# One ScalarE copy of 2048 half-words in place of a ScalarE and a VectorE copy, in the first attention of a macaron block

## The chip, the cores and the metric

The kernel runs on one core of a Trainium2 chip. The metric is the device time of one execution in microseconds (us), median of several runs. TensorE (PE in the profile) does the matmuls, VectorE (DVE), ScalarE (ACT) and GpSimd (POOL) the rest; SyncE (SP) issues most of the DMAs.

## The reference, cut to what matters

Two sequences of 1024 rows of 128 values go through two blocks, each a feed-forward, an attention and a feed-forward. The change lies in the attention of the first block: 16 heads of width 8, keys and queries turned by their position (rope), causal mask.

```
x = x + 0.5 * _L0_ffn_ref(_layernorm(x, axis=-1), ...)
x = x + _L0_attn_ref(_layernorm(x, axis=-1), L0_attn_W_KQV, L0_attn_W_O)    # here
x = x + 0.5 * _L0_ffn_ref(_layernorm(x, axis=-1), ...)
...
K, Q, V = to_heads(K), to_heads(Q), to_heads(V)
Q = _rope(Q, freqs)
K = _rope(K, freqs)
scores = jnp.einsum('bhqd,bhkd->bhqk', Q, K) / sqrt(d)
scores = jnp.where(causal, -jnp.inf, scores)
probs = jax.nn.softmax(scores, axis=-1)
heads = jnp.einsum('bhqk,bhkd->bhqd', probs, V)
```

## The kernel before, in words

The 32 heads of both sequences are worked on in 8 groups of 4 heads (`G` = 8, `key` or `g` is the group). Keys and queries are kept as 16-bit floats in `stacks`, a row of the sequence on each partition. For a group, a step `gkq` turns both with 16 TensorE transposes (line 1365), 8 for the keys into the first bank of a PSUM slot and 8 for the queries into the second. Each bank then holds 512 words of 4 bytes, that is 1024 values of 16 bits for each partition. The values leave for SBUF, to `KT` and `QT`, which lie side by side: ScalarE copies the keys (line 684, called at 793), VectorE the queries (line 1047).

After this come, for each group, 18 steps `gmax` (TensorE makes scores with queries as rows, line 1207, with the mask at line 1198; VectorE takes maxima by blocks, line 1054), one `gturn` (the maxima are turned, line 1376, and a DMA puts them among the rows of the turned queries), 18 steps `gexp` (scores with keys as rows, ScalarE takes the exponential, line 811), 9 steps `gweigh` (TensorE weighs the values, line 1156) and one `gheads`. ScalarE also saves the group's sum (`save_heads`, line 690).

Every step that needs PSUM takes the next slot of a ring of 3 slots of 2 banks (`RING`). Before it writes, TensorE waits until all the readers named in the step have read what the slot's user of three steps earlier left there. A few side steps have a bank of their own. The order of all steps is written out by hand in the string `ORDER`, where `a` is `gkq`, `m` `gmax`, `t` `gturn`, `e` `gexp`, `w` `gweigh`; every engine goes through it in this order, and nothing overtakes on an engine. It begins with `ammmmmmmmammm`. So `gkq` of group 0 is the first step, that of group 1 comes after 8 `gmax` of group 0, that of group 2 among `gmax` of group 1, and so on up to group 7. The steps `h` are the feed-forward parts and norms between the two attentions: `xt` (a transpose, copied out by ScalarE, line 684, and for some by VectorE, line 1032), `up` (line 1346; ScalarE takes a tanh, line 790, VectorE gates, lines 1042 and 1043) and others.

Some steps are preceded by idle matmuls that keep the clock up (`keep_clock`, line 1246, counts in `KEEP`). The first `gmax` of a group waits until both copies of its `gkq` are done.

After the first attention, from about 300 us on, the second attention (16 heads of width 64, in 16 pairs) and the last feed-forward parts follow in the same ring.

Of the kernel before, what the change touches and what calls it, by code (L numbers as in the profile page):

```python
# [10 lines left out]
F16 = mybir.dt.float16  # L11
# [15 lines left out]
G = B * H // GH  # L27
# [19 lines left out]
SETS = 3  # L47
# [97 lines left out]
def gated_steps(s, b):  # L145
    return (turned_norm_steps(s, b) + [("up", (s, b), (c, half), "AV") for c in range(HC) for half in range(2)]
            + [("down", (s, b), None, "V")])


def first_steps(b):  # L150
    rope = [[("rope", (b, half), k, "") for k in range(4)] for half in range(2)]
    return (int_ffn_steps(0, b) + turned_norm_steps(1, b) + [("qk", b, 0, "A")] + rope[0][:2] + [("v", b, None, "A")]
            + rope[0][2:] + [("qk", b, 1, "A")] + rope[1])


def middle_steps(b):
    return ([("acts", b, None, "A"), ("wo0", b, None, "V")] + int_ffn_steps(2, b) + gated_steps(3, b)
            + turned_norm_steps(4, b))


def streams():

    halves = [(i, u) for i in range(CH) for u in range(2)]
    return {
        "a": [("gkq", g, None, "AV") for g in range(G)],
        "m": [("gmax", g, at, "V") for g in range(G) for at in halves],
        "t": [("gturn", g, None, "A") for g in range(G)],
        "e": [("gexp", g, at, "A") for g in range(G) for at in halves],
        "w": [("gweigh", g, i, "") for g in range(G) for i in range(CH)],
        "g": [("gheads", g, None, "V") for g in range(G)],  # L170
        "Q": [("pq", p, None, "AV") for p in range(PAIRS)],
        "K": [("pk", p, None, "AV") for p in range(PAIRS)],
        "V": [("pv", p, None, "A") for p in range(PAIRS)],
        "M": [("max", p, i, "V") for p in range(PAIRS) for i in range(CH)],
        "T": [("turn", p, None, "AV") for p in range(PAIRS)],
        "E": [("exp", p, i, "A") for p in range(PAIRS) for i in range(CH)],
        "W": [("weigh", p, i, "") for p in range(PAIRS) for i in range(CH)],
        "S": [("sum", p, None, "A") for p in range(PAIRS - 1)],
        "O": [("wo", b, (0, (NP, WO_EARLY)[b], k), "V") for b in range(B) for k in range(WO_PARTS)],
        "h": (first_steps(1) + [("scale", 1, None, "V")]  # L180
              + [("wsplit", n, None, "") for n in range(3)] + middle_steps(0) + middle_steps(1) + gated_steps(5, 0)),
    }
# [12 lines left out]
    "MWMEMWMEEEKWWMEMWMEQThVEMSEMMWWWMEEMWWWMEEMWWMEEEMWWWTSEEEEWWWWEEEEEESWWOOOOEEWWWWWWW"  # L195
)
LEFT = {letter: iter(steps) for letter, steps in streams().items()}
PLAN = [next(LEFT[letter]) for letter in ORDER]
AT = {step[:3]: n for n, step in enumerate(PLAN)}
SLOT_NO = [0] + list(accumulate(int(bool(step[3])) for step in PLAN))  # L200
# [33 lines left out]
def read(e, *key):  # L234

    return READS[e][AT[key]]
# [15 lines left out]
def macaron_block_kernel(nc, x, w_kqv, w_o0, w_int, w_scale, bias, w_q, w_k, w_v, w_o1, w_gate, w_up,  # L252
# [3 lines left out]
    with ctx:  # L256
        def sb(name, shape, dt=F32):
            return ctx.enter_context(nc.sbuf_tensor(name, shape, dt))

        def sem(name):  # L260
            return ctx.enter_context(nc.semaphore(name))
# [10 lines left out]
        big = sb("big", [P, 16384])  # L272
# [42 lines left out]
               for at in (wkqv_s[0:2 * T, 2 * P:3 * P], turns[0:2 * T].rearrange("p w t d -> p (w t d)"))]  # L315
# [12 lines left out]
            "p h s d -> p (h s d)")  # L328
        KT, QT = ([big[:, 8192 + 1024 * r + 512 * w:8192 + 1024 * r + 512 * (w + 1)].bitcast(F16) for r in range(SETS)]
                  for w in range(2))  # L330
        spare = big[:, 15360:16384]
        mall = spare[:, 0:2 * GH * T * T].rearrange("p (r h t k) -> p r h t k", r=2, h=GH, t=T)
        mxn = spare[:, 512:576].rearrange("p (r h t) -> p r h t", r=2, h=GH)
# [31 lines left out]
        def slot_of(n):  # L365
            return ps[:, 6, :] if ON_SIDE[n] else banks(2 * (RING_NO.get(n, 0) % RING), 2)
# [12 lines left out]
        slot_filled, slot_act, slot_dve = sem("slot_filled"), sem("slot_act"), sem("slot_dve")  # L379
        slot_seen = {"A": slot_act, "V": slot_dve}  # L380
# [108 lines left out]
        def _(pool):  # L489
# [88 lines left out]
            g.memset(tops(1), SHIFT_TOP).then_inc(slots_set, 1)  # L578

            for n, (kind, key, arg, _) in enumerate(PLAN):  # L580
                if kind == "ln" and arg == 1:
                    s, b = key
# [94 lines left out]
        def _(act):  # L677
            a = nc.scalar
# [3 lines left out]
            def copy_out(n, dst, src):  # L682
                act.wait_ge(slot_filled, SLOT_NO[n] + 1)
                a.activation(dst, src, ACT.Copy).then_inc(slot_act, 1)  # L684
# [35 lines left out]
            def copy_heads(half):  # L720

                act.wait_ge(rope_sum, half + 1)
                for w, (at, (first, again)) in enumerate(((Ks, K_HIGH), (Qs, Q_HIGH))):
                    at = at[:, 0, :, heads[half]]
                    ins = a.activation(at[:, :, :, first], RA[half][:, :, 8 * w:8 * w + 8], ACT.Copy)
                ins.then_inc(high_done, 1)
                act.wait_ge(high_done, half + 1)
                for w, (at, (first, again)) in enumerate(((Ks, K_HIGH), (Qs, Q_HIGH))):
                    at = at[:, 0, :, heads[half]]
                    ins = a.activation(at[:, :, :, again], at[:, :, :, first], ACT.Copy)  # L730
                ins.then_inc(dups_done, 1)
# [9 lines left out]
            for n, (kind, key, arg, readers) in enumerate(PLAN):  # L741
                slot = slot_of(n)
# [47 lines left out]
                    a.activation(ffn_g[:, (2 * c + half) % 2], slot[:, 0:512], ACT.Tanh, scale=0.5 * W_SCALE).then_inc(slot_act, 1)  # L790

                if kind == "gkq":
                    copy_out(n, KT[key % SETS], slot[:, 0:512].bitcast(F16))
                    if key == 0:
                        copy_heads(1)
                        act.wait_ge(w_in, 16 * W_LOADS)
                        for k in range(3):
                            if k == 2:
                                act.wait_ge(wmax_ready, 2)
                            a.activation(ffn_h[:, k % 2], w_raw[k], ACT.Square,  # L800
                                         accum_out=wmax[1][:, k:k + 1]).then_inc(wmax_ready, 1)
# [59 lines left out]
        def _(dve):  # L861
            v = nc.vector
# [122 lines left out]
            for n, (kind, key, arg, readers) in enumerate(PLAN):  # L985
                slot = slot_of(n)
# [46 lines left out]
                if kind == "up":  # L1033
                    c, half = arg
                    dve.wait_ge(slot_act, READS["A"][n])
                    if arg == (0, 0):
                        dve.wait_ge(converted, 1)
                        before = last_before(n, "down")
                        if before is not None:
# [2 lines left out]
                    link(v.scalar_tensor_tensor(gate, gate, 1.0, slot[:, 0:512], ALU.add, ALU.mult))  # L1042
                    v.tensor_tensor(ffn_h[:, c, 512 * half:512 * half + 512], gate, slot[:, 512:1024],
                                    ALU.mult).then_inc(slot_dve, 1)
                if kind == "gkq":
                    dve.wait_ge(slot_filled, SLOT_NO[n] + 1)
                    v.tensor_copy(QT[key % SETS], slot[:, 512:1024].bitcast(F16)).then_inc(slot_dve, 1)
                if kind == "gmax":
                    i, u = arg
                    r = key % 2  # L1050
# [22 lines left out]
                if kind in ("pq", "pk"):  # L1073
                    r = key % SETS
# [3 lines left out]
                if kind == "max":  # L1078
                    r = key % 2
# [64 lines left out]
        def _(pe):  # L1144
# [57 lines left out]
            def group_scores(slot, pieces, u, still, moving, cut):  # L1202

                for q, (t, a0, a1, off) in enumerate(pieces):
                    for h in range(2):
                        rows = slice(HR * (2 * u + h), HR * (2 * u + h + 1))
                        ins = te.matmul(slot[:, 512 * h + off:512 * h + off + a1 - a0], still[rows, tile(t)],  # L1207
                                        moving[rows, a0:a1], start=q == 0, stop=cut is None and q == len(pieces) - 1)
                return ins if cut is None else cut_group(slot, u, cut)
# [78 lines left out]
            for n, (kind, key, arg, readers) in enumerate(PLAN):  # L1288
# [6 lines left out]
                slot = slot_of(n)  # L1295
# [70 lines left out]
                if kind == "gmax":  # L1366
                    i, u = arg
                    if (i, u) == (0, 0):
                        for e in "AV":
                            pe.wait_ge(slot_seen[e], read(e, "gkq", key, None))  # L1370
                    r = key % SETS
                    ins = group_scores(slot, M_PLACED[i], u, QT[r], KT[r], cutq0 if i in DIAGONAL else None)
                if kind == "gturn":
# [4 lines left out]
                if kind == "gexp":  # L1378
# [4 lines left out]
                    r = key % SETS  # L1383
# [21 lines left out]
                if kind == "max":  # L1405
                    r = key % SETS
# [9 lines left out]
                if kind == "exp":  # L1416
                    r = key % SETS
# [157 lines left out]
```

## Time and profile before

| | |
|---|---|
| time, median of 3 runs | 804.91 us (800.31 to 806.59) |
| the profiled execution's own time | 800.03 us |
| its span, first to last instruction | 798.2 us |
| mean granted clock of TensorE | 0.959 |
| busy: PE, DVE, ACT, POOL | 91%, 67%, 56%, 58% of the span |
| `gkq` steps | 8, from 35 to 243 us |

Durations below are of the one profiled execution. Its time is 1.8 us more than its span, and 4.88 us less than the median of the timed runs. The granted clock of TensorE is given as a share of 2.4 GHz: 0.5 is 1.2 GHz.

### The profile page before, as it was taken

To read this page: it belongs to the slowest core of one execution; us is meant where nothing else is said; L and a number is where in the kernel's file an instruction comes from. 1 tells how busy PE (TensorE), PEld (TensorE's weight loads), DVE (VectorE), ACT (ScalarE), POOL (GpSimd) and SP (SyncE) were. 2 spreads that over 40 slices of the span, in tenths; PEclk is the share of its full clock that TensorE was granted. 3 is DMA by queue.
4 is the path that set the end of the run, shared out by engine and by line. 5 is a ranking of instruction groups with operands and counts; after the bars stand their busy time and mean duration, and the time that the engine had idled before them with its cause. 6 is when DMAs were issued, how large, how long until landed. Compare 5 with 4: busy or idle time off the path is not lost.

```text
span 798.2 us, 21288 instructions
## 1 busy us (share of the span) xinstructions
PE 725.3 (91%) x9393; PEld 429.3 (54%) x9406; DVE 532.1 (67%) x704; ACT 450.9 (56%) x495; POOL 466.8 (58%) x367
## 2 busy tenths in 40 slices
PE   3667888888888899998999999999999999999997
PEld 1533454445335444554565565555776655676764
DVE  7699967889778765777675575556536556753037
ACT  2424769986575689555636655665444665546312
POOL 6815567600850300499968777877655986667840
PEclk9855989999899999999999999999999999999999
DMA  8000000000000000000001111001101101111110
GB/s 271 2 1 2 3 2 3 2 3 2 2 2 2 2 3 2 2 2 5 27 4 26 29 30 29 10 22 28 30 2 28 29 3 29 29 29 30 28 29 26
DMA packets 13223, 16.18 MB, mean 20 GB/s; under 512 B 3052, under 2 KB 10572, under 8 KB 13132
## 3 DMA queue, kind: packets, MB, share of 16 engines
q1 hardware_dynamic: 12556, 14.50, 6.3%
q8 instruction: 74, 1.21, 0.6%
q10 hardware_dynamic: 576, 0.33, 0.2%
q14 instruction: 17, 0.14, 0.1%
HBM read 13.26 MB, written 1.17 MB: 18 GB/s over the span
## 4 chain that ended last, share of the span: by engine, by line
PE 70%; DVE 17%; POOL 5%; ACT 5%; issue 3%; DMA 0%; ACTq 0%; POOLq 0%; DVEq 0%
PE ps L1228 19%; PE ps L1177 16%; DVE big L1054 9%; PE ps L1156 6%; PE ps L1398 5%; PE ps L1207 5%; PE ps L1435 3%; ACT Pr L811 3%; PE ps L1403 2%; PE ps L1352 2%; PE ps L1238 2%; POOL acts L672 1%; DVE moments L1004 1%; PE ps L1346 1%; PE ps L1318 1%
## 5 line engine op out<-in xcount | busy, mean ns | idle before, releaser
L1081 DVE TENSOR_REDUCE mxb<-ps 128x8 f32<-128x1024 f32 x144 | 173.3, 1222 | 90.4 <-PE ps L1228 61.3
L672 POOL TENSOR_TENSOR V0s<-V0s,Pr 128x1024 f32<-128x1024 f32 x77 | 182.1, 2365 | 62.7 <-ACT Pr L840 31.0
L1054 DVE TENSOR_REDUCE big<-ps 128x8 f32<-128x1024 f32 x144 | 168.9, 1218 | 27.9 <-PE ps L1207 16.6
L811 ACT ACTIVATE Pr<-ps,exp_scale 128x1024 f32<-128x1024 f32 x144 | 154.8, 1114 | 44.4 <-PE ps L1207 31.5
L840 ACT ACTIVATE Pr<-ps,exp_scale 128x1024 f32<-128x1024 f32 x112 | 119.5, 1114 | 90.3 <-PE ps L1228 72.9
L1228 PE MATMUL ps<-big 64*128 64x128 f16 (+2 forms) x2560 | 168.9, 259 | 0.7 <-DVE mxb L1081 0.4
L1207 PE MATMUL ps<-big 32*128 32x128 f16 (+2 forms) x1280 | 102.4, 279 | 35.7 <-DVE big L1054 22.2
L1228 PEld LDWEIGHTS ps<-big 64*128 64x128 f16 x2560 | 92.8, 94 | 71.6 <-issue 17.0
L1177 PE MATMUL ps<-Pr,V1s 128*64 128x128 f32 (+2 forms) x960 | 111.3, 371 | 0.0
L1207 PEld LDWEIGHTS ps<-big 32*128 32x128 f16 x1280 | 40.4, 95 | 108.5 <-DVE big L1054 53.1
L587 POOL TENSOR_TENSOR stats<-moments 128x8 f32<-128x8 f32 x9 | 1.9, 210 | 163.7 <-DVE moments L1004 163.7
L684 ACT ACTIVATE big<-ps 128x1024 f16<-128x1024 f32 (+3 forms) x63 | 51.9, 826 | 71.0 <-PE ps L1398 28.2
L672 POOL TENSOR_TENSOR acts<-acts,Pr 128x1024 f32<-128x1024 f32 x35 | 82.5, 2357 | 13.2 <-ACT wkqv_s L823 4.0
L1156 PE MATMUL ps<-Pr,V0s 128*18 128x128 f32 (+2 forms) x1280 | 82.1, 382 | 0.2 <-ACT Pr L690 0.2
L1177 PEld LDWEIGHTS ps<-Pr,V1s 128*64 128x64 f32 x960 | 56.0, 136 | 37.1 <-issue 24.7
L1077 DVE TENSOR_TENSOR big<-ps,big 128x1024 f16<-128x1024 f32 x32 | 39.1, 1223 | 34.4 <-ACT big L684 33.6
L1228 PE MATMUL ps<-big,shr_s 64*128 64x256 f16 (+2 forms) x384 | 55.8, 287 | 0.0
L518 POOL TENSOR_TENSOR big<-Pr,rec_b 128x1024 f32<-128x1024 f32 x15 | 35.5, 2363 | 17.6 <-DMA rec_b<-scratch_dram 7.5
L1398 PE MATMUL ps<-XT,wqkv 128*128 128x512 f16 x192 | 45.3, 380 | 0.0
L1156 PEld LDWEIGHTS ps<-Pr,V0s 128*18 128x18 f32 x1280 | 30.4, 100 | 20.2 <-issue 13.2
L840 ACT ACTIVATE V0s<-ps,exp_scale 128x1024 f32<-128x1024 f32 x22 | 24.5, 1114 | 18.2 <-PE ps L1218 17.0
L1398 PEld LDWEIGHTS ps<-XT,wqkv 128*128 128x128 f16 x192 | 17.6, 98 | 22.0 <-ACT Pr L840 1.7
(242 smaller groups left out, 921.7 us busy)
## 6 DMA issues: line engine op xcount, KB each, us to landing
rec_b<-scratch_dram SPq DMA_DIRECT2D x30, 256.0 KB, 3.9
X<-in_x_dram SPq DMA_DIRECT2D x2, 256.0 KB, 3.8
big<-in_pick_rows_dram SPq DMA_DIRECT2D x2, 256.0 KB, 3.0
X<-in_x_dram SPq DMA_DIRECT2D x1, 512.0 KB, 5.4
rec_b<-in_w_q_dram SPq DMA_DIRECT2D x1, 512.0 KB, 5.8
XT<-in_w_k_dram SPq DMA_DIRECT2D x1, 512.0 KB, 6.6
XT<-in_w_v_dram SPq DMA_DIRECT2D x1, 512.0 KB, 7.3
wo_s<-in_w_o_dram SPq DMA_DIRECT2D x1, 512.0 KB, 8.1
```

The source lines that it names most:

```text
L672: g.tensor_tensor(dst, dst, src, ALU.add).then_inc(summed, 1)
L684: a.activation(dst, src, ACT.Copy).then_inc(slot_act, 1)
L811: a.activation(group_buf[e_no % GROUP_BUFS], by_head(slot), ACT.Exp, scale=exp_scale[0][:, 0:1]).then_inc(slot_act, 1)
L840: a.activation(dst, by_head(slot), ACT.Exp, scale=exp_scale[1][:, 0:1]).then_inc(slot_act, 1)
L1054: v.tensor_reduce(maxima_of(mall[:, r, 2 * u:2 * u + 2], i), block_view(by_head(slot), i), AX.X, ALU.max, negate=True).then_inc(slot_dve, 1)
L1077: v.tensor_tensor(low, slot, high, ALU.subtract).then_inc(slot_dve, 1)
L1081: v.tensor_reduce(maxima_of(mxb[:, r], arg), block_view(by_head(slot), arg), AX.X, ALU.max, negate=True).then_inc(slot_dve, 1)
L1156: ins = te.matmul(ps[HR * j:HR * j + 2 * VW, 7, a0 - 512 * half:a1 - 512 * half], values(g // GB, t, GH * (g % GB) + j, half), src, start= ...
L1177: ins = te.matmul(ps[h * D1:(h + 1) * D1, 6 + bank, a0 - 512 * bank:a1 - 512 * bank], V1[p % SETS][:, t, h * D1:(h + 1) * D1], src, start= ...
L1207: ins = te.matmul(slot[:, 512 * h + off:512 * h + off + a1 - a0], still[rows, tile(t)], moving[rows, a0:a1], start=q == 0, stop=cut is Non ...
L1228: ins = te.matmul(slot[:, 512 * h + off:512 * h + off + a1 - a0], still[rows], moving[rows], start=q == 0 and k == 0, stop=not goes_on and ...
L1398: ins = te.matmul(slot[:, cols], w16[:, ww], x16[:, xx, cols], start=part == 0, stop=part == 2)
```

## The change

ScalarE copies the whole slot of a `gkq`, both banks, in one instruction to `KQT`, which is `KT` and `QT` of the same buffer taken as one piece. VectorE's copy is dropped, `gkq` has one reader, and the first `gmax` of a group waits for ScalarE's semaphore only. The words of the title are of 4 bytes; the instruction's elements are of 16 bits, so it goes from 1024 elements for each partition to 2048.

```
-        "a": [("gkq", g, None, "AV") for g in range(G)],
+        "a": [("gkq", g, None, "A") for g in range(G)],
...
+        KQT = [big[:, 8192 + 1024 * r:8192 + 1024 * (r + 1)].bitcast(F16) for r in range(SETS)]
...
                 if kind == "gkq":
-                    copy_out(n, KT[key % SETS], slot[:, 0:512].bitcast(F16))
+                    copy_out(n, KQT[key % SETS], slot.bitcast(F16))
...
-                if kind == "gkq":
-                    dve.wait_ge(slot_filled, SLOT_NO[n] + 1)
-                    v.tensor_copy(QT[key % SETS], slot[:, 512:1024].bitcast(F16)).then_inc(slot_dve, 1)
...
                     if (i, u) == (0, 0):
-                        for e in "AV":
-                            pe.wait_ge(slot_seen[e], read(e, "gkq", key, None))
+                        pe.wait_ge(slot_act, read("A", "gkq", key, None))
```

## Rows read from the trace of the kernel before

**Rows 1.** The page: busy time by engine, and the chain that ended last.

```profile
PE 725.3 (91%) x9393; PEld 429.3 (54%) x9406; DVE 532.1 (67%) x704; ACT 450.9 (56%) x495; POOL 466.8 (58%) x367
PE 70%; DVE 17%; POOL 5%; ACT 5%; issue 3%; DMA 0%; ACTq 0%; POOLq 0%; DVEq 0%
```

**Rows 2.** Windows: stretch, its length, busy us of each engine, granted clock.

```profile
300.00:798.00 498.00, 485.83 (x6051) 300.12 (x6050) 289.61 (x360) 261.76 (x279) 339.01 (x194) 1.00 0.08 20
...
36.00:71.40 35.40, 22.46 (x235) 11.31 (x234) 33.95 (x40) 10.25 (x17) 8.61 (x12) 0.54 0.01 1
71.40:300.00 228.60, 199.27 (x3007) 104.92 (x3017) 183.35 (x240) 168.66 (x176) 92.89 (x104) 0.94 0.01 2
```

**Rows 3.** ScalarE's copies out of PSUM by shape, then VectorE's of the queries.

```profile
L684 ACT ACTIVATE big<-ps 128x512 f32<-128x512 f32 x15 | 9.0, 599 | 14.9 <-PE ps L1238 14.9
L684 ACT ACTIVATE big<-ps 128x1024 f16<-128x1024 f16 x8 | 8.2, 1028 | 9.4 <-PE ps L1365 9.4
...
L1047 DVE COPY big<-ps x8: 679/688/692, 36.3 to 242.3; 128x1024 f16<-128x1024 f16 x8
```

**Rows 4.** Timeline at group 0: start, length, engine, line.

```profile
36.25 1.06 ACT L684 ACTIVATE big<-ps 128x1024 f16<-128x1024 f16 x1
36.25 0.69 DVE L1047 COPY big<-ps 128x1024 f16<-128x1024 f16 x1 [1.16 <-PE ps L1365]
...
37.37 0.40 PE L1207 MATMUL ps<-big 32*128 32x128 f16 x8 [1.16 <-ACT big L684]
```

**Rows 5.** Timeline at group 1, each engine from its own answer.

```profile
46.79 1.79 PE L1207 MATMUL ps<-big 32*128 32x512 f16 x8
...
46.90 1.02 ACT L684 ACTIVATE big<-ps 128x1024 f16<-128x1024 f16 x1 [3.90 <-PE ps L1365]
...
47.09 0.68 DVE L1047 COPY big<-ps 128x1024 f16<-128x1024 f16 x1
47.69 11.40 DVE L1054 TENSOR_REDUCE big<-ps 128x8 f32<-128x1024 f32 x10
```

**Rows 6.** Timeline at group 2.

```profile
73.52 1.61 PE L1207 MATMUL ps<-big 32*128 32x256 f16 x8 [0.40 <-ACT Pr L811]
...
71.44 1.02 ACT L684 ACTIVATE big<-ps 128x1024 f16<-128x1024 f16 x1 [3.54 <-PE ps L1365]
```

**Rows 7.** Timeline at group 3.

```profile
106.10 1.09 PE L1318 MATMUL ps<-id_s,D 128*128 128x128 f32 x8 [0.47 <-ACT Pr L811]
...
104.02 1.02 ACT L684 ACTIVATE big<-ps 128x1024 f16<-128x1024 f16 x1 [0.45 <-PE ps L1365]
```

**Rows 8.** Timeline at group 4.

```profile
142.22 0.39 PE L1207 MATMUL ps<-big 32*128 32x512 f16 x2
142.97 0.64 PE L1207 MATMUL ps<-big 32*128 32x256 f16 x6 [0.37 <-DVE big L1054]
...
141.14 1.03 ACT L684 ACTIVATE big<-ps 128x1024 f16<-128x1024 f16 x1
142.04 4.14 ACT L811 ACTIVATE Pr<-ps,exp_scale 128x1024 f32<-128x1024 f32 x4
```

**Rows 9.** Timeline at group 5.

```profile
168.48 0.39 PE L1207 MATMUL ps<-big 32*128 32x512 f16 x2 [0.56 <-ACT big L684]
```

**Rows 10.** Timeline at group 6.

```profile
212.66 0.61 PE L1246 MATMUL ps<-cutq_s,shr_s 128*128 128x512 bf16 x2
...
211.50 2.11 ACT L811 ACTIVATE Pr<-ps,exp_scale 128x1024 f32<-128x1024 f32 x2
```

**Rows 11.** Timeline at group 7.

```profile
244.14 0.60 ACT L790 ACTIVATE ffn_g<-ps 128x512 f32<-128x512 f32 x1
...
244.78 0.68 DVE L1042 SCALAR_TENSOR_TENSOR ffn_g<-ffn_g,ps 128x512 f32<-128x512 f32 x1
```

**Rows 12.** Windows where the clock falls.

```profile
200.00:205.00 5.00, 3.04 (x42) 1.28 (x40) 5.00 (x8) 1.94 (x3) 4.00 (x10) 0.76 0.01 3
205.00:210.00 5.00, 5.00 (x54) 1.92 (x47) 3.71 (x6) 2.79 (x3) 4.51 (x8) 0.55 0.00 0
```

## The prediction

> **What bounds the kernel now.** I read the page first: TensorE is busy for 91% of the span and holds 70% of the chain that ended last, VectorE 17%, ScalarE 5% [rows 1]. That is an average over unlike stages, so the windows come next. From 300 us on TensorE is busy 485.83 of 498.00 us at full clock, and no `gkq` lies there: the change can reach that part only by starting it later or earlier. Up to 71.4 us VectorE is the bound (33.95 of 35.40 us, TensorE at about half clock, 0.54), and ScalarE does little (10.25 us). Between 71.4 and 300 us three engines hand work to each other through a ring of three slots: TensorE 199.27, VectorE 183.35, ScalarE 168.66 of 228.60 us [rows 2]. None is full there, so what counts is not the sum of an engine's work but how long each slot is held and which wait ends last at each of the eight `gkq`. I therefore read the timelines around each of them, engine by engine, with the ring's order beside it.
>
> **The price of the two copies.** The title counts words, the instruction counts elements. ScalarE takes 599 ns for 512 elements of 4 bytes (512 words) and 1028 ns for 1024 elements of 2 bytes (also 512 words) [rows 3]. The same words cost 1.7 times as much, so ScalarE is paid by the element. The slope is (1028 - 599) / 512 = 0.838 ns for an element. The new copy has 2048 elements: 1028 + 1024 x 0.838 = 1886 ns, that is 0.86 us more than now. Eight of them put 6.9 us on ScalarE. VectorE loses 8 x 0.688 = 5.5 us [rows 3]. This isn't an even exchange, and it also ends the overlap: today the halves run at once and the slot is free after the longer, 1.03 us; afterwards after 1.89 us. No shape in the trace has 2048 elements; bounds for the lengthening are 0 (if words counted) and 1.03 us (a second whole copy with its fixed part). I take 0.86, by the slope between the two nearest rows.
>
> On this exchange the Trainium skill (ScalarE: Activation LUTs, Rules for kernel authors) says that elementwise work belongs on VectorE, which for 16-bit values is up to about three times faster per element. The rows show 688 against 1028 ns, a ratio of 1.5, for a source in PSUM [rows 3]. By the page's ratio the copy dropped would have been worth only 0.34 us each to VectorE, 2.7 us in all, and by the row 5.5 us; the rule speaks against the change either way.
>
> **Group by group.** In each case: who was waited for, and what the copy's 0.86 us more or VectorE's 0.69 us less does to that.
>
> Group 0. Both copies start at 36.25, VectorE is done at 36.94, ScalarE at 37.31, and TensorE's first scores start at 37.37, released by ScalarE [rows 4]. There is nothing else for TensorE or for the maxima. Plus 0.86 us in full. The heads' copies and the squares behind it on ScalarE come later by as much, but ScalarE has room (10.25 of 35.40 us) [rows 2].
>
> Group 1, in the stretch bound by VectorE. Its copy sits between two maxima, from 47.09 to 47.77, and the next maxima start at 47.69 in the merged row [rows 5]. Without the copy the next one would wait for TensorE: the scores after the transposes start at 46.79 and their 8 matmuls are three steps in 1.79 us, 0.6 us each at half clock, so the first is there at 47.40. With a semaphore's 0.05 us VectorE starts at 47.45 instead of 47.77: a gain of 0.32, not of 0.69. ScalarE's copy would end at 46.90 + 1.89 = 48.79; the step that takes this slot is then ready at 49.4, and VectorE wants it at 47.45 + 2 x 1.14 = 49.73 (10 maxima in 11.40 us [rows 5]). So the longer copy is hidden here, by 0.3 us. Minus 0.32 us.
>
> Group 2. ScalarE copies at 71.44 to 72.46 [rows 6]; behind it is the exponential of 1.1 us whose end frees the slot that TensorE waits for, and TensorE resumes at 73.52, released by ScalarE. The copy is in the line without a gap. Plus 0.86.
>
> Group 3. ScalarE copies at 104.02, then does two exponentials, and TensorE's transposes of the feed-forward start at 106.10 after an idle 0.47, released by the first of these [rows 7]. ScalarE is first in, first out; its own next copy needs these transposes. Plus 0.86.
>
> Group 4. VectorE held the wait: scores start at 142.97, released by a maximum. But ScalarE goes from the copy at 141.14 straight into four exponentials without a gap, and the scores at 142.22 start as the copy's end frees the slot [rows 8]. With the copy's end at 143.02 these scores start at 143.1. The step after them needs the first exponential's end, 143.15 before and 144.0 after, and the weighing that followed at 143.54 stands behind it. VectorE's gain is lost behind this. Of 0.86 some 0.05 was slack: plus 0.8.
>
> Group 5. TensorE's scores start at 168.48, after an idle 0.56, released by the copy itself [rows 9]; the slot is free 0.86 later. Plus 0.86.
>
> Group 6. ScalarE's exponentials start at 211.50, right behind the copy, and TensorE's clock keepers and scores at 212.66, when the first of them (1.1 us) is over [rows 10]. Plus 0.86.
>
> Group 7. ScalarE does the copy, one exponential and then the first tanh at 244.14, over at 244.74, and VectorE's first gate starts at 244.78 [rows 11]. Today VectorE reaches it at the same moment, 244.8; without its copy it would be there at 244.1, but the tanh would end at 245.6. The chain of gates then runs on VectorE alone. Plus 0.8.
>
> Five groups at 0.86 are 4.3; with 0.8 + 0.8 - 0.32 the sum is **plus 5.6 us**. Against the profiled execution's own time this is 800.03 + 5.6 = 805.6. The median of the runs lies 4.88 us above that execution, so in the metric it is 804.91 + 5.6 = 810.5 us. After 300 us the busy TensorE neither gives it back nor adds to it. One semaphore less to wait for at the first maxima costs and saves nothing visible, since the later of the two decided anyway. No DMA is moved: SyncE's wait before the shift rows is on a later step of ScalarE. If ScalarE is late there by 0.86 as well, that is the same delay and not a second one. Bounds of the sum: each ScalarE wait that is on the path at 0 to 1.03 us, so from minus 0.3 to plus 6.8 us, before any effect on the clock.
>
> **The rivals.**
>
> *The clock falls once or twice more.* TensorE's idle time grows by the 5.6 us, in pieces just where it waits already. The windows show what a low clock costs: granted 0.76 from 200 to 205 and 0.55 from 205 to 210 us, after TensorE had been busy only 3.04 of 5 us; it then worked without a gap [rows 12]. Half clock there lasted (0.24 x 5 + 0.45 x 5) / 0.5 = 6.9 us, and of it about 6 us in full work, in which 3 us are lost. For it: group 6 lies right behind this fall, and the clock between 71.4 and 300 us is 0.94 on average, so falls are at hand [rows 2]. Against: their places may shift either way, and where VectorE sets the pace, as up to 71.4 us, half clock takes nothing. One or two more give 5.6 + 3 = 8.6 to 5.6 + 6 = 11.6, so 813.5 to 816.5. It decides as soon as one gap turns a full-clock stretch into such a half-clock one.
>
> The Trainium skill (TensorE: Matmul & The Clock Gate, Two states) says that the half clock is the default and steady activity lifts it; by it longer waits can only harm. The rows at 200 to 210 agree as far as they go [rows 12].
>
> *Slack takes the delays up: not slower.* The mechanism is VectorE's queue. If at groups 2 to 7 VectorE is the engine waited for next, its 0.69 us less lets it catch up what ScalarE's copy delays. For it: VectorE is busy 183.35 of 228.60 us, more than ScalarE [rows 2], and at group 4 a maximum was the releaser [rows 8]. Against: after groups 2, 3, 5 and 6 the wait ends with ScalarE. If it took all six back and gained 0.2 each, the sum is 0.86 - 0.32 - 1.2 = -0.7, so 804.2; half of that is 2 to 3 us, 807.5. It decides where the next maximum ends more than 0.86 us after ScalarE's work.
>
> *ScalarE copies by the word.* Then the new copy takes some 1.03 us, nothing is longer, and VectorE's 0.32 at group 1 and up to 0.69 at groups 4 and 7 come off: minus 0.3 to 1.7, 803.2 to 804.6. The two lengths for 512 words speak plainly against it [rows 3].
>
> **How the numbers follow.** The forecast's case (807.5 to 813) gets 0.57, more low clock (813 and above) 0.24, slack taken up 0.14, copies by the word or another gain 0.05. A measurement of this kernel can hardly tell under 1% from nothing, that is 8 us: below 796.9 is faster, above 813.0 slower. Faster: 0.04, some luck with the clock in the last two cases. Slower: 0.24, the clock's. Within: 0.72. The range has to leave out 2 in 10: from 804.2, where slack takes nearly all, to 816.5, where two more falls of the clock are paid.
>
> **What would show it in the profile after.** ScalarE's line 684 of the `gkq` shape with 2048 elements at 1.88 us; 1.03 would make the price wrong. VectorE's busy time lower by 5.5 and ScalarE's higher by 6.9 us. TensorE's first scores at about 38.2 instead of 37.37. Group 2's `gkq` 0.5 later than now (0.86 less 0.32), group 7's 4.8 later (the sum without its own term), and 300 us of before reached about 5.6 us later, with the stretch behind it as long as now. The clock in the windows from 71 to 300: 0.94 as now, lower if the rival holds. What would make the prediction wrong above all is the clock: a longer gap can tip it in stretches of several us, and my sum counts each group's delay as if the pattern after it stayed.

## The result and the profile after

The changed kernel takes 810.31 us (median of 20 runs) against 804.84 us (median of 20 runs of the kernel before beside them): ratio 1.0079, 95% interval 1.0062 to 1.0095. The forecast was 810.5 us. That the longer copy is the cause is shown below; how much of the loss is plain delay and how much the clock stays partly open. One of the changed kernel's 20 runs took 1383.16 us, and one each of two partial versions below 1381.86 and 1380.13 us, all with a granted clock of 1.0; these three are left out of every ratio, mean and range here, and without its own the changed kernel's median is 810.00 us.

The profiled execution after took 815.85 us. That is near the upper end of the changed kernel's runs (804.86 to 816.22 us), as the one of before, 800.03 us, was at the lower end of its own (800.14 to 806.65). Subtracting one from the other would give 15.8 us, nearly three times the difference of the medians. So the profile after is read here for its local waits, and the sums are made over many runs. The page, busy time by engine and the chain that ended last:

```profile
PE 739.7 (91%) x9406; PEld 435.8 (54%) x9406; DVE 527.9 (65%) x696; ACT 457.7 (56%) x495; POOL 466.7 (57%) x367
...
PE 74%; DVE 15%; ACT 5%; issue 3%; POOL 2%; DMA 0%; ACTq 0%; DVEq 0%; POOLq 0%
```

Beside [rows 1]: VectorE has 8 instructions and 4.2 us less, ScalarE as many instructions and 6.8 us more. ScalarE's copies by shape (the group of line 685, which is line 684 of before):

```profile
L685 ACT ACTIVATE big<-ps 128x2048 f16<-128x2048 f16 x8 | 15.0, 1881 | 8.3 <-PE ps L1363 8.3
...
L685 ACT ACTIVATE big<-ps 128x512 f32<-128x512 f32 x15 | 9.0, 599 | 14.9 <-PE ps L1236 14.8
```

1881 ns for 2048 elements, where the slope of [rows 3] gave 1886. The windows of the changed kernel, cut at the group 2 copy and 498 us before the end:

```profile
36.00:71.76 35.76, 22.62 (x233) 11.19 (x233) 32.78 (x38) 11.57 (x16) 8.37 (x12) 0.54 0.01 2
71.76:315.90 244.14, 213.27 (x3018) 111.48 (x3016) 180.31 (x234) 174.13 (x177) 92.80 (x104) 0.88 0.01 2
315.90:814.00 498.10, 485.62 (x6050) 300.13 (x6048) 289.58 (x360) 261.49 (x279) 338.92 (x194) 1.00 0.08 20
```

Against [rows 2], the last 498 us are the same to 0.2 us of TensorE's work: nothing is given back or added there. Nearly all of the difference of this execution lies between 71 and 316 us, 228.60 us before and 244.14 now, and the granted clock there is 0.88 instead of 0.94. The section on the clock below comes back to this.

The waits at single groups are the forecast ones. Timelines of TensorE, ScalarE and VectorE at groups 0 and 1, then of TensorE at groups 2, 3, 4, 5 and 6, each with what ended its idle time:

```profile
37.95 0.40 PE L1205 MATMUL ps<-big 32*128 32x128 f16 x8 [2.01 <-ACT big L685]
...
35.98 1.92 ACT L685 ACTIVATE big<-ps 128x2048 f16<-128x2048 f16 x1
...
49.41 0.62 PE L1205 MATMUL ps<-big 32*128 32x256 f16 x8 [0.99 <-ACT big L685]
...
48.02 6.88 DVE L1052 TENSOR_REDUCE big<-ps 128x8 f32<-128x1024 f32 x6 [0.27 <-PE ps L1205]
...
73.69 0.60 PE L1205 MATMUL ps<-big 32*128 32x512 f16 x2 [0.99 <-ACT big L685]
...
107.19 0.39 PE L1205 MATMUL ps<-big 32*128 32x512 f16 x2 [0.38 <-ACT big L685]
108.20 1.09 PE L1316 MATMUL ps<-id_s,D 128*128 128x128 f32 x8 [0.61 <-ACT Pr L812]
...
146.76 0.40 PE L1205 MATMUL ps<-big 32*128 32x512 f16 x6 [0.79 <-ACT big L685]
147.76 0.39 PE L1205 MATMUL ps<-big 32*128 32x512 f16 x2 [0.61 <-ACT Pr L812]
...
176.22 0.39 PE L1205 MATMUL ps<-big 32*128 32x512 f16 x2 [1.38 <-ACT big L685]
...
220.74 0.60 PE L1244 MATMUL ps<-cutq_s,shr_s 128*128 128x512 bf16 x2 [0.83 <-ACT big L685]
```

The chain that ended last goes through the copy at group 2, without a gap on ScalarE until TensorE resumes:

```profile
71.76 1.88 ACT big L685
73.64 1.01 ACT Pr L812
74.70 1.61 PE ps L1205 x8
```

At group 0 TensorE's idle time is 2.01 us instead of 1.16 [rows 4]: plus 0.85. At group 1 VectorE's copy is gone, but its next maxima wait 0.27 us for TensorE. From VectorE's first maximum of group 0 to the first one behind its old copy of group 1 it was 9.66 us (38.03 to 47.69, the latter in [rows 5]) and is 9.41 now (38.61 to 48.02): a gain of 0.25, and TensorE's 0.99 for the long copy is hidden, since VectorE's six maxima run on without a gap (6.88 us). At group 5 the idle time ended by the copy is 1.38 instead of 0.56 [rows 9], at group 4 the releaser of 142.97 was a maximum [rows 8] and is now ScalarE. At group 0 and at groups 2 to 6 these are the steps of the prediction; at group 1 the gain is a little smaller. Up to the copy of group 2 the sum fits too: from the first copy to the third it was 35.19 us (36.25 to 71.44) and is 35.78 (35.98 to 71.76), 0.59 more where 0.86 less 0.32 was forecast.

Group 7 differs. VectorE, then ScalarE, TensorE:

```profile
256.18 0.69 DVE L1043 SCALAR_TENSOR_TENSOR ffn_g<-ffn_g,ps 128x512 f32<-128x512 f32 x1 [1.93 <-ACT ffn_g L791]
...
255.55 0.60 ACT L791 ACTIVATE ffn_g<-ps 128x512 f32<-128x512 f32 x1 [0.80 <-PE ps L1344]
...
253.79 5.31 PE L1344 MATMUL ps<-XTF,wg_s 128*128 128x512 f16 x16 [0.81 <-ACT big L685]
```

From the start of the copy to the first gate it is 2.8 us before (241.98 to 244.78) and 4.3 us now (251.86 to 256.18). 0.85 of it is the copy. The other 0.7 us go to TensorE: from the start of its matmuls, which the copy releases, to the first tanh it is 1.76 us (253.79 to 255.55), where it was 1.08 in the trace of before (243.06 to 244.14). The windows of this place go with that: the granted clock (third number from the end) is no longer full, where the kernel before had 1.00 from 240 to 250 us:

```profile
250.00:255.00 5.00, 3.48 (x40) 2.29 (x37) 3.29 (x6) 4.74 (x4) 0.00 (x0) 0.90 0.00 0
255.00:260.00 5.00, 5.00 (x22) 1.52 (x20) 3.42 (x6) 2.39 (x4) 0.00 (x0) 0.76 0.00 0
```

### The profile page after: what moved, and what is told of

The parts are those of the page before. It is cut to its first block, busy times and chain, and to the rows that moved or that the text cites. A ratio compares the mean times of both kernels' runs of the same rounds, so it can differ in the third digit from the quotient of the medians.

```text
span 814.1 us, 21282 instructions
## 1 busy us (share of the span) xinstructions
PE 739.7 (91%) x9406; PEld 435.8 (54%) x9406; DVE 527.9 (65%) x696; ACT 457.7 (56%) x495; POOL 466.7 (57%) x367
## 4 chain that ended last, share of the span: by engine, by line
PE 74%; DVE 15%; ACT 5%; issue 3%; POOL 2%; DMA 0%; ACTq 0%; DVEq 0%; POOLq 0%
PE ps L1226 19%; PE ps L1175 16%; DVE big L1052 8%; PE ps L1154 7%; PE ps L1205 6%; PE ps L1395 5%; PE ps L1432 3%; ACT Pr L812 3%; PE ps L1400 2%; PE ps L1350 2%; PE ps L1236 2%; PE ps L1344 2%; DVE moments L1005 1%; ACT big L685 1%; PE ps L1216 1%
## 5 line engine op out<-in xcount | busy, mean ns | idle before, releaser
L1052 DVE TENSOR_REDUCE big<-ps 128x8 f32<-128x1024 f32 x144 | 169.2, 1219 | 44.3 <-PE ps L1205 26.4
L685 ACT ACTIVATE big<-ps 128x1024 f16<-128x1024 f32 (+3 forms) x63 | 58.8, 935 | 70.4 <-PE ps L1395 28.2
L1154 PE MATMUL ps<-Pr,V0s 128*18 128x128 f32 (+2 forms) x1280 | 85.1, 393 | 0.2 <-ACT Pr L691 0.2
```

The costliest lines, as they stand in the source:

```text
L1052: v.tensor_reduce(maxima_of(mall[:, r, 2 * u:2 * u + 2], i), block_view(by_head(slot), i), AX.X, ALU.max, negate=True).then_inc(slot_dve, 1)
L1154: ins = te.matmul(ps[HR * j:HR * j + 2 * VW, 7, a0 - 512 * half:a1 - 512 * half], values(g // GB, t, GH * (g % GB) + j, half), src, start= ...
```

## The clock, run by run

Every run lists its span and mean granted clock, so its time at half clock can be worked out: 2 x (1 - clock) x span, since half clock counts as 0.5. Over 29 runs of the kernel before (the ones beside the first four experiments) and 19 of the changed one, which were not run side by side:

| | runs | mean time | mean clock | time at half clock |
|---|---|---|---|---|
| before | 29 | 804.44 | 0.9527 | 76.0 |
| after | 19 | 810.67 | 0.9492 | 82.2 |

The same kernel before takes 800.04 us in a run with clock 0.959 and 807.02 in one with 0.949. A line through its runs rises by 0.33 us for each us at half clock, one through the changed kernel's by 0.40, with a rest of 0.9 and 0.7 us. At 75 us of half clock both lines give 804.1 and 807.8. So of the 6.2 us between the means about 3.7 remain at equal clock, and about 2.5 go with 6 us more at half clock. This is a fit and not an experiment. It doesn't tell whether the clock's fall or the longer time comes first, and the runs of before in the two later sets give slopes of 0.37 and 0.20 and 804.0 and 804.5 us at 75. In the runs below "half clock" is this figure, averaged over the kernel's runs.

## Experiments

All are timed in five rounds beside the kernel before on the same chip, in three sets on three chips. The kernel before has a mean of 804.44 us (76.0 us at half clock) in the first set, which are the first four experiments, 803.83 (74.6) beside groups 2, 3, 5, 6, groups 4, 7 and the idle matmuls, and 804.94 (77.4) beside groups 0, 1 and the last version. A mean is compared with its own set; the changed kernel's 810.67 stands beside none of them, so against it the ratios count.

**Which half of the exchange.** In the changed kernel VectorE spends its old time all the same:

```
+                if kind == "gkq":
+                    dve.wait_ge(slot_filled, SLOT_NO[n] + 1)
+                    v.tensor_reduce(stats[:, 10, 0:1], cutq0.rearrange("p j c -> p (j c)"), AX.X, ALU.max)
```

> The changed kernel, and VectorE spends the time of its old copy all the same: at each gkq it reduces 512 constant 16-bit values to one unused value (some 0.7 us), signals nobody and nobody waits for it. It separates the two halves of the exchange. My theory (the longer copy on ScalarE is the price, VectorE's relief is worth only 0.3 us at group 1, as TensorE isn't ready sooner): within 0.3 to 1 us of the changed kernel, ratio to before 1.0075 to 1.010. Rival, VectorE's relief pays back much of ScalarE's delay at groups 2 to 7: then its loss shows as 2 us or more over the changed kernel, ratio 1.011 or more.

Measured: ratio 1.0121 (1.0088 to 1.0155), mean 813.72 us over 6 runs, 90.4 us at half clock. The reduction takes as long as the old copy:

```profile
L1048 DVE TENSOR_REDUCE stats<-cutq_s 128x1 f32<-128x512 bf16 x8 | 5.4, 679 | 1.2 <-PE ps L1366 1.2
```

The mean is 3.0 us above the changed kernel's (3.4 by the ratios), where I had said 0.3 to 1; by that it is the rival's. The intervals of the two ratios overlap, and at 75 us of half clock this kernel's line gives 807.8 us, the same as the changed kernel's. So the relief may work through the clock and not through the maxima. With six runs and a fit this isn't settled.

**Is it the copy's length?** One copy by ScalarE still, but as 4-byte words:

```
-        KQT = [big[:, 8192 + 1024 * r:8192 + 1024 * (r + 1)].bitcast(F16) for r in range(SETS)]
+        KQT = [big[:, 8192 + 1024 * r:8192 + 1024 * (r + 1)] for r in range(SETS)]
...
-                    copy_out(n, KQT[key % SETS], slot.bitcast(F16))
+                    copy_out(n, KQT[key % SETS], slot)
```

> The changed kernel with the same one copy, but read and written as 1024 values of 4 bytes instead of 2048 of 2 bytes. [...] If ScalarE is paid by the element, the copy takes 1.03 us instead of 1.88, no group is delayed any more, group 1 gains its 0.3 us and groups 4 and 7 up to 0.7 us each: 0.3 to 1.7 us under before, ratio 0.998 to 1.000. If instead it is the single reader or the loss of two engines at once that costs, and not the copy's length, it stays at about 1.007.

Measured: 1.0002 (0.9980 to 1.0025), mean 804.38 us, 75.9 us at half clock. The copy takes 1.02 us at group 0, and TensorE waits 1.12 us for it, as before the change:

```profile
37.03 1.02 ACT L685 ACTIVATE big<-ps 128x1024 f32<-128x1024 f32 x1 [0.65 <-PE ps L1363]
...
38.11 0.61 PE L1205 MATMUL ps<-big 32*128 32x128 f16 x8 [1.12 <-ACT big L685]
```

This is the cleanest of the runs. The only difference from the changed kernel is the length of eight copies, 8 x 0.86 = 6.9 us on ScalarE, and it takes away 6.3 us of mean time (6.2 by the ratios), all of the loss, with the clock's share in it. And the difference from the kernel before is that VectorE doesn't copy: that is worth next to nothing, between a gain of 1.6 and a loss of 2.0 us by the interval. I had allowed it a gain of up to 1.7.

**Shorter than before.** The kernel before (keys by ScalarE, queries by VectorE), with ScalarE's half as 512 words of 4 bytes instead of 1024 values of 2:

```
-                    copy_out(n, KT[key % SETS], slot[:, 0:512].bitcast(F16))
+                    copy_out(n, big[:, 8192 + 1024 * (key % SETS):8704 + 1024 * (key % SETS)], slot[:, 0:512])
```

> [...] Its copy should take 0.60 us instead of 1.03, VectorE's stays 0.69. By my theory every group but 1 is paced by ScalarE's copy or by what stands behind it: group 0 gains 0.35 us (VectorE's copy is next), groups 2, 3, 5 and 6 0.34 to 0.43 each, 4 and 7 up to 0.3: 2.0 to 2.7 us under before, ratio 0.997. The rival with slack (VectorE paces the groups from 2 on): 0.35 us in all, ratio 0.9995.

Measured: 0.9976 (0.9956 to 0.9996), mean 802.24 us: 2.2 us under before (1.9 by the ratio) at nearly the same half clock, 75.6 us, at the lower end of my theory's 2.0 to 2.7 and away from the other's 0.35, which the interval just reaches. ScalarE's copy is 0.60 us, and at group 0 the releaser is now VectorE:

```profile
37.23 0.60 ACT L684 ACTIVATE big<-ps 128x512 f32<-128x512 f32 x1 [0.88 <-PE ps L1365]
...
38.07 0.40 PE L1207 MATMUL ps<-big 32*128 32x128 f16 x8 [0.88 <-DVE big L1047]
```

**The mirror.** VectorE alone copies the slot, `v.tensor_copy(KQT[key % SETS], slot.bitcast(F16))`, ScalarE nothing:

> The mirror of the change: VectorE copies the whole slot, ScalarE nothing. VectorE's copy of 2048 values should take 1.1 to 1.4 us (688 ns for 1024). The slot is free 0.2 us later than before, not 0.86, and ScalarE's exponentials behind it come 0.9 us sooner. Group 0 plus 0.2, group 1 plus 0.5 to 0.6 (VectorE paces it), groups 3 and 6 up to minus 0.8 each, 2 and 5 minus 0.3 to plus 0.2, 4 and 7 plus 0.5: near 0, ratio 0.998 to 1.002. If VectorE were the engine that paces the groups, as the rival with slack has it, plus 3 to 4 us, ratio 1.004 to 1.005.

Measured: 0.9995 (0.9974 to 1.0016), mean 803.86 us, 70.9 us at half clock. The copy is 1.22 us:

```profile
L1047 DVE COPY big<-ps 128x2048 f16<-128x2048 f16 x8 | 9.8, 1219 | 2.8 <-PE ps L1365 2.7
```

VectorE, the busier engine of the two in this stage, takes the whole copy at no measurable loss; ScalarE, the less busy one, at a loss of 6 us with the long copy and of none with the short one (1.0002). Part of VectorE's result goes with 5 us less at half clock; at 75 us this kernel's line gives 804.9 us, 0.8 above before. The busy share didn't tell this; how long the copy holds the slot and the queue behind it did.

**The groups by themselves.** `gkq` is done in the new way in some groups and in the old way in the others (`"A" if g in WHOLE else "AV"`, and so at each place of the diff). Groups 2, 3, 5 and 6:

> The change in groups 2, 3, 5 and 6 alone, where my prediction had ScalarE's queue end the wait; the others copy as before. Prediction's sum: 4 x 0.86 = 3.4 us, ratio 1.0043. If slack or VectorE's relief takes the delay up: 1.5 us or less, ratio 1.002 or less. If the direct delay is as predicted and the clock adds its share on top (the changed kernel ran 82 us at half clock on average against 76, at 0.3 to 0.4 us a us): 5 us, ratio 1.006.

Measured: 1.0036 (1.0014 to 1.0058), 2.9 us by the ratio and 3.6 by the means (807.40 us), against 3.4 predicted. 78.7 us at half clock instead of 74.6. Groups 4 and 7:

> The change in groups 4 and 7 alone, where VectorE's copy was on the chain before and the prediction had ScalarE take its place at once: 2 x 0.8 = 1.6 us, ratio 1.002. Rival: VectorE's relief counts there, and the two together give 0 or a gain, ratio 0.999 to 1.000.

Measured: 1.0020 (0.9987 to 1.0053), 1.6 us by the ratio and 1.9 by the means (805.74 us), against 1.6 predicted. The interval doesn't exclude the rival. Groups 0 and 1:

> The change in groups 0 and 1 alone. Prediction: plus 0.86 and minus 0.32, together 0.54 us, ratio 1.0007. The parts tried so far (2, 3, 5, 6: means 3.0 us over before; 4, 7: 1.3 us) leave 1.9 of the changed kernel's 6.2 us of mean difference; if the parts add up, groups 0 and 1 cost 1.9 us, ratio 1.0024, and then something beside the two waits is in it, the clock first of all.

Measured: 0.9989 (0.9971 to 1.0006). By the ratio that is 0.9 us less than before, where the prediction's sum is 0.54 more, just outside the interval (its upper end is 0.5), and a share of 1.9 more is excluded. The parts' ratios add up to 0.36 + 0.20 - 0.11 = 0.45% or 3.6 us; the whole is 0.79% or 6.4 us. The four intervals together (1.8, 2.7, 1.4 and 1.3 us to either side) give some 3.7 us for the gap of 2.8. So whether the parts add up is not settled.

The traces of these runs tell more where two kernels have the same clock between the copies of two groups. Windows from copy to copy: groups 3 to 4 with the old copy (groups 0, 1 changed) and with the long one (groups 2, 3, 5, 6 changed); then groups 4 to 5, old (groups 0, 1 changed) and long (groups 4, 7 changed); then groups 6 to 7, with the one short copy by words of the second experiment and with the long one (groups 2, 3, 5, 6):

```profile
105.84:142.26 36.42, 30.36 (x452) 17.47 (x450) 28.45 (x35) 30.81 (x36) 23.76 (x15) 1.00 0.01 2
105.69:142.95 37.26, 30.43 (x452) 17.47 (x449) 27.73 (x34) 31.66 (x35) 23.75 (x15) 1.00 0.01 2
...
142.26:168.50 26.24, 23.96 (x413) 12.47 (x413) 23.66 (x27) 22.57 (x25) 11.70 (x5) 1.00 0.01 3
140.87:167.97 27.10, 23.49 (x413) 12.29 (x413) 23.20 (x26) 23.43 (x24) 11.71 (x5) 1.00 0.01 3
...
213.47:246.17 32.70, 28.34 (x398) 12.75 (x397) 22.45 (x34) 23.86 (x24) 18.29 (x24) 0.90 0.01 2
213.33:246.38 33.05, 28.97 (x401) 12.65 (x398) 22.53 (x34) 24.72 (x24) 18.36 (x24) 0.90 0.01 2
```

At group 3 the long copy costs 0.84 us and at group 4 0.86: the forecast price, with no slack behind it. At group 6, at a clock of 0.90 in both, only 0.35 remains when the copy of group 7 comes.

**Idle matmuls against the clock.** In `KEEP`, 7 idle matmuls ahead of `('gmax', 0, (0, 0))` and 2 each ahead of the second step after `gkq` of groups 2, 3, 4, 5 and 7, in the changed kernel. Group 6 was meant too, but its step, `('gexp', 4, (5, 1))`, stands again further down in `KEEP` with the old count of 1, and the later entry counts.

> The changed kernel with idle matmuls of 512 columns where TensorE is about to wait for the copy: 7 ahead of the first gmax of group 0, 2 each ahead of the second step after the gkq of groups 2 to 7 (group 1 has none). If a part of the change's price is the clock, time at half clock falls from 82 to 76 us or less and the ratio to before from 1.008 to 1.003 to 1.005. If it is delay alone, the clock's share stays and the keepers cost up to 0.2 us each where they stand in the way: 1.008 to 1.010.

Measured: 1.0062 (1.0035 to 1.0089), mean 808.67 us, 70.9 us at half clock instead of 82.2. And in the kernel before:

> The same idle matmuls in the kernel before, as the control: if they help the kernel before as much as the changed one, their gain says nothing of the change. Clock's share of the change as above: here at most 1 us either way, ratio 0.999 to 1.001. If the clock is a loss of its own that both kernels have: 0.996 or less.

Measured: 1.0027 (0.9997 to 1.0057), mean 805.94 us, 71.7 us at half clock instead of 74.6. Both misses: the changed kernel didn't come down to 1.005, and before went up by more than 1 us (2.1 by the means). In the changed kernel the ratio fell by 0.17% or 1.4 us. The difference of the two effects, 3.5 us, has the sign of a clock's share in the change, but the traces show another cause for much of it. TensorE at group 0, first the kernel before with idle matmuls, then the changed one:

```profile
36.08 1.67 PE L1253 MATMUL ps<-cutq_s,shr_s 128*128 128x512 bf16 x7
37.68 0.40 PE L1214 MATMUL ps<-big 32*128 32x128 f16 x8
...
36.03 1.67 PE L1251 MATMUL ps<-cutq_s,shr_s 128*128 128x512 bf16 x7
38.20 0.40 PE L1212 MATMUL ps<-big 32*128 32x128 f16 x8 [0.50 <-ACT big L692]
```

In the changed kernel they end before the long copy does and cost nothing: 1.97 us from the start of the copy to the first scores, as without them. In the kernel before they outlast the short copy: 1.40 us instead of 1.12. The same comparison, from the start of the copy to the work behind it, gives 0.56 us more at group 2, 0.31 at group 3, 0.42 at group 4, none at group 5 and 0.62 at group 7 in the kernel before, some 2.2 us with group 0, and nothing at groups 0 and 2 to 5 in the changed one. So the control carries a cost that the changed kernel doesn't, and the pair of runs doesn't isolate the clock. What it does show is that 11 us less at half clock brought the changed kernel only 1.4 us (2.0 by the means): less than half of what its line promises. Part of the clock was won where it is worth nothing. From the first copy to the third VectorE sets the pace, and the stretch takes 35.78 us at a clock of 0.54 (35.98 to 71.76) and with the idle matmuls at 0.58 (36.23 to 72.01).

**The better version.** Words throughout, and the whole slot by ScalarE in groups 1, 4 and 7:

```
+WHOLE = (1, 4, 7)
...
+                    if key in WHOLE:
+                        copy_out(n, KQT[key % SETS], slot)
+                    else:
+                        copy_out(n, KQT[key % SETS][:, 0:512], slot[:, 0:512])
```

> Copies by 4-byte words throughout: in groups 1, 4 and 7, where VectorE's copy was on the chain, ScalarE copies the whole slot as 1024 words (1.03 us); in the others it copies the keys as 512 words (0.60 us) and VectorE the queries. [...] Over the kernel with every group split by words (ratio 0.9976): 0.3 us less at group 1, nothing to 0.3 at 4 and 7, ratio 0.997. If VectorE's relief is worth nothing, as the kernel with one copy of 1024 words showed (1.0002), and ScalarE's 0.4 us more counts at 4 and 7: 0.9985.

Measured: 0.9960 (0.9943 to 0.9977), mean 801.69 us: 3.2 us less than before by the ratio, the lowest ratio of all versions. From the version with every group split by words (0.9976) it can't be told apart.

## Why the prediction was right, point by point

*The price.* Right: 1881 ns for the forecast 1886, and the rival that ScalarE copies by the word is out. A slope between two shapes of the trace held at twice the larger one. The trap was the unit: 1024 words of two values each are 2048 elements.

The Trainium skill's rule that VectorE is up to three times faster for such work (ScalarE: Activation LUTs, Rules for kernel authors) holds here in its direction; of its factor, an upper limit, half was seen: 2048 values took 1219 ns on VectorE and 1881 on ScalarE, 1.5 times.

*Group by group.* The local steps are in the profile after nearly as predicted: plus 0.85 at group 0, ScalarE as the releaser at groups 2 to 6, and at group 1 minus 0.25 with the long copy hidden. The 0.32 forecast there counted from the end of VectorE's copy (47.77), though the row has the next maximum starting at 47.69; from that it is 0.24. As sums, groups 2, 3, 5 and 6 measured 2.9 to 3.6 us against 3.4, and 4 and 7 1.6 to 1.9 against 1.6, with intervals of 1.8 and 2.7 us to either side. Groups 0 and 1 came out at minus 0.9 against plus 0.54, which lies just outside the interval, though up to group 2 the profile after shows 0.59. At equal clock groups 3 and 4 cost the forecast 0.84 and 0.86 us, group 6 only 0.35 of its 0.86.

*The sum.* 5.6 us were forecast; 5.5 by the medians and 6.4 by the ratio were measured. But it may be right partly by luck. By the fit the delays are 3.7 us at equal clock, and the 6 us more at half clock bring some 2.5. Then the weak step is the sentence that the pattern after each delay stays, with the clock left out of the likeliest case: I had given the clock to a rival only, at 3 us for each fall, as if it came in whole pieces, and it came as a small share in the mean, 0.9492 instead of 0.9527 granted. The sum would then hold two errors of some 2 us with opposite signs, the slack behind group 6 being one piece of the first. The idle matmuls speak for a smaller share: at the 1.4 to 2.0 us that they brought for 11 us, 6 us are worth about 1 us, by this estimate, and the delays would be near the 5.6. How the loss divides between delay and clock is not shown; that both go back to the length of the copy is (1.0079 against 1.0002).

*VectorE's relief.* I took it as 0.3 us and the rival with slack as up to 6. With the copy's length kept (words) it is nothing, with 2 us to either side. With the long copy it may be 3 us, by one kernel run six times, and perhaps through the clock. How the relief should act on the clock is open.

*The rivals.* "Slack takes the delays up": not so in full, the two parts without groups 0 and 1 measured 4.5 us by their ratios where 5.0 was forecast, and groups 3 and 4 kept all of theirs. "The clock falls once or twice more": time at half clock did rise, but whatever share of the loss is its own, it is under the 3 to 6 us of that rival. *VectorE's busy time* fell by 4.2 us on the page, not by the 5.5 I named. Neighbours in its queue overlap: the copy at group 1 ends at 47.77 and the next maximum starts at 47.69 [rows 5]. So a copy filled some 0.6 us of its own, eight of them 4.8, and the rest I can't place.

## What to carry to other kernels

When a copy moves from two engines to one, price it by the element type it is issued with, and then ask two things at each place: how much longer the buffer is held, and what stands behind it in that engine's queue. Busy shares were no guide here: the engine with more idle time was the wrong one to load with 1.88 us at a time, and did no harm with 1.02. Where 16-bit values leave PSUM unchanged, a ScalarE copy by 4-byte words took little over half the time; whether every pair of 16-bit values comes through unchanged when it is read as a 4-byte float was not tried. And an idle matmul that fills a wait in one kernel can stand in the way in its control, where the wait is shorter.

## What the runs showed of the hardware

The length of a ScalarE copy follows the element count and not the bytes: 512 words took 0.60 us as 512 elements and 1.03 us as 1024, 1024 words 1.02 and 1.88 us. VectorE copied 1024 16-bit values in 0.69 and 2048 in 1.22 us. One and the same kernel spreads over 7 us between executions, 800.04 to 807.02 in 29, and its mean granted clock with it, from 0.959 down to 0.948; a single profile against a single profile is then worth little below 1%.
